# Splitting the last layer's values on GpSimd, so that eleven sums over adj run as three float32r passes

## The reference, cut to what matters

```python
h = jnp.maximum(_layernorm(x, axis=-1), 0.0)
# W: (3, 128, 128)
h = jnp.einsum('bjf,kfo->kbjo', x, W)             # three values per node; x is the h above
out = (jnp.einsum('ij,bjo->bio', adj_0, h[0])     # adj_0: the diagonal
     + jnp.einsum('ij,bjo->bio', adj_1, h[1])     # adj_1: triu(adj, 1)
     + jnp.einsum('ij,bjo->bio', adj_2, h[2]))    # adj_2: tril(adj, -1)
return out + bias[None, None, :]
```

## Time and profile before

| what | value |
|---|---|
| median of 3 runs | 405.15 us |
| the profiled execution's own time | 404.75 us |
| its span, first to last instruction | 402.8 us |
| TensorE matmul busy | 396.2 us (98%) |
| VectorE busy | 346.2 us (86%) |
| ScalarE busy | 287.3 us (71%) |
| GpSimd busy | 41.0 us (10%) |
| granted TensorE clock | 1.000 |

### The profile page before, as it was taken

The page is one execution under the profiler, slowest core; times in us unless marked ns, Lnnn a source line. Parts: engine busy times, 40 slices in busy tenths (PEclk is TensorE's granted clock), DMA queues, the critical chain, the costliest instruction groups (busy, mean ns, idle before and its releaser), DMA issues.

```text
span 402.8 us, 6585 instructions
## 1 busy us (share of the span) xinstructions
PE 396.2 (98%) x2404; PEld 348.0 (86%) x2404; DVE 346.2 (86%) x872; ACT 287.3 (71%) x579; POOL 41.0 (10%) x43
## 2 busy tenths in 40 slices
PE   8999999999999999999999999999999999999997
PEld 8787889898887889899777879899797788989896
DVE  6568999997989898887998898989798979787897
ACT  4767775685798676777689676777689767766554
POOL 4910003000200003000110000300030000000130
PEclk9999999999999999999999999999999999999999
DMA  7920000000000000000000000000000000000003
GB/s 229 317 110 2 1 0 2 1 2 0 2 1 2 27 28 0 28 0 2 3 0 26 28 0 28 0 28 1 2 2 26 0 28 26 2 26 2 1 2 130
DMA packets 5215, 11.18 MB, mean 28 GB/s; under 512 B 1088, under 2 KB 2112, under 8 KB 4672
## 3 DMA queue, kind: packets, MB, share of 16 engines
q1 hardware_dynamic: 5184, 10.77, 7.6%
HBM read 6.57 MB, written 4.19 MB: 27 GB/s over the span
## 4 chain that ended last, share of the span: by engine, by line
PE 81%; DVE 13%; ACT 5%; issue 1%; POOL 0%; DVEq 0%; ACTq 0%; POOLq 0%
PE PS L514 11%; PE PS L523 11%; PE PS L515 10%; PE PS L546 6%; PE PS L543 6%; PE PS L542 6%; PE PS L592 4%; PE PS L440 4%; PE PS L463 4%; PE PS L473 4%; PE PS L455 4%; PE PS L581 3%; PE PS L582 2%; PE PS L583 2%; ACT GT L849 2%; ACT TC L855 2%
## 5 line engine op out<-in xcount | busy, mean ns | idle before, releaser
L849 ACT ACTIVATE GT<-PS,BG 128x256 f32<-128x256 f32 (+2 forms) x312 | 157.8, 563 | 16.5 <-PE PS L546 12.4
L514 PE MATMUL PS<-HH,WIH 128*128 128x256 f32 (+2 forms) x312 | 107.3, 345 | 1.8 <-DVE HH L1000 1.7
L515 PE MATMUL PS<-HH,WIL 128*128 128x256 f32 (+2 forms) x312 | 102.7, 330 | 0.0
L523 PE MATMUL PS<-HL,WIH 128*128 128x256 f32 (+2 forms) x294 | 97.3, 331 | 0.5
L855 ACT ACTIVATE TC<-CS 128x512 f32<-128x512 f32 (+2 forms) x88 | 45.2, 514 | 49.5 <-DVE CS L976 36.2
L514 PEld LDWEIGHTS PS<-HH,WIH 128*128 128x128 f32 x312 | 58.8, 188 | 11.5 <-DVE HH L1007 4.3
L382 POOL TENSOR_TENSOR RS<-VE,NHALF 128x4 f32<-128x4 f32 (+2 forms) x17 | 29.2, 1718 | 351.0 <-DVE VE L921 272.7
L515 PEld LDWEIGHTS PS<-HH,WIL 128*128 128x128 f32 x312 | 58.9, 189 | 3.9 <-issue 1.2
L523 PEld LDWEIGHTS PS<-HL,WIH 128*128 128x128 f32 x294 | 55.5, 189 | 6.6 <-DVE HL L1015 2.4
L546 PE MATMUL PS<-SL,WHH 128*128 128x256 f32 (+2 forms) x192 | 60.1, 313 | 0.1
L542 PE MATMUL PS<-SH,WHH 128*128 128x256 f32 (+2 forms) x192 | 59.9, 312 | 0.0
(11 more groups left out here) (97 smaller groups left out, 657.5 us busy)
## 6 DMA issues: line engine op xcount, KB each, us to landing
out_tbd<-X SPq DMA_DIRECT2D x15, 256.0 KB, 2.0
X<-x_tbd SPq DMA_DIRECT2D x3, 1024.0 KB, 13.2
X<-x_tbd SPq DMA_DIRECT2D x4, 256.0 KB, 4.2
WI<-wih_t SPq DMA_DIRECT2D x1, 1024.0 KB, 6.1
WH<-whh_t SPq DMA_DIRECT2D x1, 768.0 KB, 7.6
out_tbd<-X SPq DMA_DIRECT2D x2, 128.0 KB, 1.7
WL<-w_l SPq DMA_DIRECT2D x1, 192.0 KB, 6.7
WG<-wg SPq DMA_DIRECT2D x2, 64.0 KB, 3.4
```

Of the source, the lines that this page charges most:

```text
L514: pe.matmul(dst, WIH[:, p - 1, cols], x_high, start=True, stop=False)
L515: pe.matmul(dst, WIL[:, p - 1, cols], x_high, start=False, stop=False)
L523: mm = pe.matmul(dst, WIH[:, p - 1, cols], x_low, start=False, stop=(j == 0))
L849: act.activation(GT[:, s, q, 0:n], bank(s, q)[:, 0:n], ACT.Tanh if q == C else ACT.Sigmoid, bias=BG[:, 4 * (p - 1) + q:4 * (p - 1) + q + 1 ...
```

## The change

In the eleven quads for which `sums_split` is true (all of groups 0 and 1, quads 0 to 2 of group 2), the values of sides 1 and 2 are split by GpSimd into a float32r high part VH (a copy) and a low part VL (value minus high), value by value after its copy out of PSUM. The triangles of adj are split once in the same way into ADJH and ADJL. A SUM then is six float32r matmuls of 512 columns (high by ADJH and by ADJL for both sides, then low by ADJH for both sides) instead of two float32 ones. It waits for `value_high` of the quad's last value before the first four and for `value_low` before the last two. In GpSimd's order, eleven splits stand before the `rstd` of the first layer and five behind it; in the last group twelve splits stand before the four `rstd` calls. The triangles are built later, after ScalarE's and VectorE's late weight split, since ADJ2 now lies in a free part of WI; BIASH lies in VH. The other five quads stay plain float32.

```diff
+def sums_split(g, q):
+    return g < GROUPS - 2 or (g == GROUPS - 2 and q < LAST)
+def splits_before(g, n):
+    return G * g + n
+SPLIT_FIRST = 11
...
-            pool.wait_ge(consts, 4)
             pool.wait_ge(w_adj, 16)
-            for k, sign in enumerate((1, -1)):
-                pool.affine_select(out=ADJ2[:, k, :], in_=ADJ[:, :], ...)
             pool.wait_ge(w_ih, 16)
...
+            pool.wait_ge(consts, 4)
+            pool.wait_ge(late_low, LATE_ORDER.index("wi") + 1)
+            for k, sign in enumerate((1, -1)):
+                pool.affine_select(out=ADJ2[:, k, :], in_=ADJ[:, :], ...)
+            pool.wait_ge(consts, 6)
+            pool.tensor_copy(ADJH[:, :, :], ADJ2[:, :, :]).then_inc(side_parts, 1)
+            pool.wait_ge(side_parts, 1)
+            pool.tensor_tensor(ADJL[:, :, :], ADJ2[:, :, :], ADJH[:, :, :].bitcast(F32),
+                               ALU.subtract).then_inc(side_parts, 1)
+            def split_value(g, n):
+                full, high, low = value_sides(n)
+                pool.wait_ge(value_sb, G * g + n + 1)
+                pool.tensor_copy(high, full).then_inc(value_high, 1)
+                pool.wait_ge(value_high, splits_before(g, n) + 1)
+                pool.tensor_tensor(low, full, high.bitcast(F32), ALU.subtract).then_inc(value_low, 1)
             def group(i):
+                for n in range(SPLIT_FIRST) if i > 0 else ():
+                    split_value(i - 1, n)
                 rstd(VE1, var1, 2 * (QUARTERS + i + 1), RS1, rs1, 0, G)
+                for n in range(SPLIT_FIRST, G) if i > 0 else ():
+                    split_value(i - 1, n)
...
             i = GROUPS - 1
+            for n in range(LAST * PACK):
+                split_value(i - 1, n)
             for q in range(QUADS):
...
             def last_sum(g, q, ps, lo=0, hi=PACK):
+                if not sums_split(g, q):
+                    for k in range(SIDES):
+                        last_side(g, q, k, ps, lo, hi)
+                    return
+                pe.wait_ge(value_high, splits_before(g, q * PACK + hi))
                 for k in range(SIDES):
-                    last_side(g, q, k, ps, lo, hi)
+                    high = VH[:, k, lo * D:hi * D]
+                    pe.matmul(ps[:, lo * D:hi * D], ADJH[:, k, :], high, start=(k == 0), stop=False)
+                    pe.matmul(ps[:, lo * D:hi * D], ADJL[:, k, :], high, start=False, stop=False)
+                pe.wait_ge(value_low, splits_before(g, q * PACK + hi))
+                for k in range(SIDES):
+                    mm = pe.matmul(ps[:, lo * D:hi * D], ADJH[:, k, :], VL[:, k, lo * D:hi * D],
+                                   start=False, stop=(k == SIDES - 1))
+                mm.then_inc(out_mm, 1)
```

More of the change, by code:

```diff
@@ L190, in program @@
         ADJ = sb("ADJ", [T, T])
-        ADJ2 = sb("ADJ2", [T, SIDES, T])
+        ADJH = sb("ADJH", [T, SIDES, T], F32R)
+        ADJL = sb("ADJL", [T, SIDES, T], F32R)
+        VH = sb("VH", [T, SIDES, PACK * D], F32R)
+        VL = sb("VL", [T, SIDES, PACK * D], F32R)
         DIAG = sb("DIAG", [T, 1])
@@ L201, in program @@
         BIAS = sb("BIAS", [T, D])
-        BIASH = sb("BIASH", [T, D], F32R)
         BIAS2 = sb("BIAS2", [T, D], F32R)
@@ L220, in program @@
         NHALF = sb("NHALF", [T, G])
+        ADJ2 = WI[:, POOL_SKIPS, 0:SIDES * T].rearrange("p (k t) -> p k t", k=SIDES)
+        BIASH = VH[:, 0, 0:D]
         PS = ctx.enter_context(nc.psum_tensor("PS", [128, 8, 512], F32))
@@ L275, in program @@
         value_sb = sem("value_sb")
+        side_parts = sem("side_parts")
+        value_high = sem("value_high")
+        value_low = sem("value_low")
         own_ready = sem("own_ready")
@@ L314, in values, with value_sides @@
             return (WI, WH)[q % 2]
+        def value_sides(n):
+            q, b = divmod(n, PACK)
+            cols = slice(b * D, b * D + D)
+            return values(q)[:, 1:PARTS, cols], VH[:, :, cols], VL[:, :, cols]
         def quad(q):
@@ L389, in _ @@
                 pool.tensor_tensor(SHIFT1[:, part], MINUS1[:, part], RS1[:, part], ALU.mult).then_inc(shift1, 1)
-            pool.wait_ge(consts, 4)
             pool.wait_ge(w_adj, 16)
-            for k, sign in enumerate((1, -1)):
-                pool.affine_select(out=ADJ2[:, k, :], in_=ADJ[:, :], compare_op=ALU.is_gt, fill=0.0,
-                                   base=0, pattern=[[-sign, T]], channel_multiplier=sign).then_inc(consts, 1)
             pool.wait_ge(w_ih, 16)
@@ L412, in _ @@
                     done += 1
+            pool.wait_ge(consts, 4)
+            pool.wait_ge(late_low, LATE_ORDER.index("wi") + 1)
+            for k, sign in enumerate((1, -1)):
+                pool.affine_select(out=ADJ2[:, k, :], in_=ADJ[:, :], compare_op=ALU.is_gt, fill=0.0,
+                                   base=0, pattern=[[-sign, T]], channel_multiplier=sign).then_inc(consts, 1)
+            pool.wait_ge(consts, 6)
[9 more added lines that the diff above has]
+                pool.tensor_tensor(low, full, high.bitcast(F32), ALU.subtract).then_inc(value_low, 1)
             def group(i):
+                for n in range(SPLIT_FIRST) if i > 0 else ():
+                    split_value(i - 1, n)
                 rstd(VE1, var1, 2 * (QUARTERS + i + 1), RS1, rs1, 0, G)
+                for n in range(SPLIT_FIRST, G) if i > 0 else ():
+                    split_value(i - 1, n)
                 for s in range(STREAMS):
@@ L672, in _ @@
             pe.wait_ge(bias_parts, 3)
+            pe.wait_ge(side_parts, 2)
             for i in range(1, GROUPS - 1):
```

## The result

The changed kernel takes 414.46 us (median; 414.21 to 414.67), the kernel before 405.05 us beside it: ratio 1.0233, 95% interval 1.0222 to 1.0243. Slower by 9.4 us, where +4.2 us were forecast. The span grew from 402.8 to 412.6 us, and the granted clock is 1.0 in both.

A forecast was written before the change was run, and what follows sets the result against it. TensorE was taken as the bound on average (98% busy), partly waiting for VectorE. Delays of 2.85 + 1.05 + 1.0 less 0.7 gained gave +4.2 us: 408.95, as a median 409.4 us; range 402.8 to 414.0.

The forecast's parts named there:

- the triangles: adj's later triangles on GpSimd fall into group 0, needed by TensorE some 50 us later: no cost.
- value 11: Split at 256.5 to 257.7, held back by the pow, where VectorE runs gapless into unit 13's chain: 1.0 us lost.
- rival C: VectorE pays full price, whole-instruction turns, 0.9 us and more a value: +11, 416 us; chance 0.05.
- The price of a value: VectorE delay per split value from GpSimd's streaming: 0.65 x 0.81 = 0.5 us.
- SUM -1's gain: Shorter float32r sum on TensorE's path, twice 0.35 us: 0.7 us gained, kept because it comes ahead of the delays.
- the late chain behind SUM 1: Value 7's split runs beside VectorE's L1015 and L1072, delaying L967, the chain's head: 0.35 x 3 = 1.05 us lost.
- values 0 to 3: Splits between 212.3 and 218.5 delay VectorE's L1063, which VALUE 4 waits for: 2.85 us lost over three groups.
- Rival B: GpSimd always yields, some 2.5 us a value, so TensorE waits in SUM 0 for the low part: about 411; chance 0.08.
- The other values meet units whose hidden parts are 2 us early: 0: Splits of values outside the named places were to delay nothing TensorE waits for: 0 us.
- The undisturbed CAST at 253.72: VectorE's CAST kept its usual 0.34 us during GpSimd's 128x16 pow; taken as evidence against whole-instruction blocking and rival C.

The follow-up runs named there:

- the run with the last quads: Changed kernel with triangles split early, but only values 12 to 15 of the first two groups split and only their two closing sums in three passes: 405.61 us.

## Why the prediction was wrong

The direction held, and that VectorE is what is held back, and three of the terms. What failed is the placing of these delays: the forecast set the values that it did not name (4 to 6, 8 to 10 and 12 to 15) and the triangles at nothing, and value 11 at half. The time, 414.46 us, lies nearer to rival C (416) than to the forecast (409.4), and C's mechanism, turns by whole instructions, is the one that the traces show, at 0.5 us a value and not C's 0.9. Point by point:

- **The price of a value: right.** "0.5 us of VectorE delay a value" was taken; VectorE's busy time grew by 22.2 / 44 = 0.50 us. The reason given (the streaming parts overlap 65% of the time) was not what happens. The engines take turns by whole instructions, and what a turn costs goes by how far apart two starts happen to be; that the two come to the same number is luck.
- **SUM -1's gain, the late chain behind SUM 1, values 0 to 3: right** (-0.7, 1.05 and 2.85 forecast; -0.7, 1.2 and 3.1 measured). TensorE also waited some 0.36 us (by the starts) in front of SUM 0 for the high part of value 3, which was to be 0.3 us early: GpSimd was slowed as well, and a value took it 1.5 us on average (1.21 to 2.00), not 1.2. Rival B was there, in small, but this wait added nothing: behind SUM 0, VALUE 4 still waits for VectorE's L1118, and in the run with the splits alone, where no sum waits, the delay from TURN 1 to VALUE 4 grows by the same 0.65 us. The changed kernel, TensorE and then VectorE:

```profile
223.34 0.47 PE L648 MATMUL PS<-VH,ADJH 128*128 128x512 f32 x1 [0.20 <-POOL VH L446]
...
225.97 0.41 PE L623 MATMUL PS<-WLH,HTH 128*128 128x384 f32 x1 [0.29 <-DVE HTL L1118]
...
225.15 0.68 DVE L1118 SCALAR_TENSOR_TENSOR HTL<-PS,HTH 128x512 fp32r<-128x512 f32 x1
```

- **"The other values meet units whose hidden parts are 2 us early: 0" failed**, and is the largest part: 1.9 + 1.3 = 3.2 us. It looked only at the hidden parts and not at what else TensorE asks of VectorE. At gate F of unit 6 it waits for ADD 0, which frees SUM 0's bank. The changed kernel, VectorE and then TensorE:

```profile
227.72 0.89 DVE L1136 SCALAR_TENSOR_TENSOR X<-WI,DIAG,X 128x512 f32<-128x512 f32 x1
228.52 1.23 DVE L1019 TENSOR_TENSOR CS<-GT 128x512 f32<-128x512 f32 x1
229.67 0.68 DVE L1145 TENSOR_TENSOR X<-PS,X 128x512 f32<-128x512 f32 x1
...
230.41 0.50 PE L556 MATMUL PS<-HH,WIH 128*128 128x512 f32 x1 [0.36 <-DVE X L1145]
```

  The add itself keeps its 0.68 us. What delays it is queued in front of it: 0.15 + 0.54 us on two instructions beside value 4's split. And at the end of a group the delay from values 12 to 15 stays in the loop between VectorE and ScalarE until the next group's layers, where TensorE has no slack, as the run with the last quads shows.
- **Value 11: right place, half the size** (1.0 forecast, 2.3 measured, for two groups). The split comes right behind the `pow`, so do VectorE's two scalings of L982, which waited for the same `pow`. The changed kernel:

```profile
263.26 0.50 POOL L446 CAST VH<-WI 128x256 fp32r<-128x256 f32 x1
263.84 0.74 POOL L448 TENSOR_TENSOR VL<-WI,VH 128x256 fp32r<-128x256 f32 x1
...
263.42 1.24 DVE L982 TENSOR_SCALAR H<-X,MINUS,RS 128x128 f32<-128x128 f32 x2
264.59 0.49 DVE L1058 TENSOR_TENSOR HF<-GT,TC 128x336 f32<-128x336 f32 x1
...
265.51 0.38 PE L556 MATMUL PS<-HH,WIH 128*128 128x256 f32 x1 [0.48 <-DVE HH L1062]
```

  The pair took 0.60 us before. It pays for the copy and for the subtraction: 0.64 us. An average price was used where the two engines were started by the same event, which makes the collision certain. The other 0.5 us of each group's 1.15 arise in the chain behind it; no run isolated them, and their cause stays open.
- **The triangles "cost none": failed by 0.6 us.** TensorE does not need them for long, but VectorE's chain runs beside them: HT 0.66 us (0.51 before) and the CAST behind it 0.74 (0.33). The run with early triangles gave back 0.60. The changed kernel there:

```profile
56.57 0.40 POOL L437 CAST ADJH<-WI 128x256 fp32r<-128x256 f32 x1
57.05 0.86 POOL L439 TENSOR_TENSOR ADJL<-WI,ADJH 128x256 fp32r<-128x256 f32 x1
...
56.67 0.66 DVE L1058 TENSOR_TENSOR HT<-GT,TC 128x336 f32<-128x336 f32 x1
57.36 0.74 DVE L1062 CAST SH<-HT 128x336 fp32r<-128x336 f32 x1
```

- **The undisturbed CAST at 253.72 was misread.** It was the argument against whole-instruction turns, and so for giving rival C only 0.05. The CAST ran inside a `pow` on 16 columns. The same CAST in the changed kernel takes 0.74 us beside the triangles' split, so it can be held. What that `pow` shows is only that a 3.09 us instruction over 16 columns does not hold it; why not, no run here settles. It was a poor stand-in for an instruction that reads 256 columns.

The sum: 3.2 (other values) + 1.3 (value 11) + 0.6 (triangles) + 0.5 (small excesses of the terms that held, start and end) = 5.6 us, the 9.8 of the ledger less the 4.2 forecast.

## What to carry to other kernels

An idle GpSimd is not free for work that reads SBUF while a VectorE that reads SBUF is near the path: count the extra VectorE time (here 0.5 us for each 1.1 us of GpSimd work), and then lay it at every place where TensorE waits for anything of VectorE, a freed bank or the next layer included, not only at the chain that the profile shows as late. What costs is the length of one reading instruction against the gap between VectorE's starts: copies of 0.40 us were nearly free (88 of them, two a value: 405.99 us), a subtraction of 0.73 was not. Before moving work to a second engine, ask whether the event that starts it also starts the engine it disturbs.

## What the runs showed of the hardware

- GpSimd's copies and subtractions take turns with VectorE's products, casts and scalings from SBUF to SBUF, by whole instructions: VectorE's 128x512 product ends 0.54 to 0.56 us after GpSimd's instruction does, for instructions of 0.48, 0.69 and 0.80 us, with one input or two. VectorE's statistics (279 ns) were not held inside a subtraction, nor anything inside the `pow` on 16 columns (3.09 us).
- GpSimd's writes take no turn that VectorE feels: with 44 memsets of 0.72 us the kernel took 404.18 us.
- VectorE's instructions with an input in PSUM kept 0.68 us beside all of this (six started inside a half subtraction with about 0.40 us of it left); its CAST from SBUF to SBUF did not (0.33 to 0.74 us at worst).
- Halving GpSimd's instructions spares VectorE (834 to 759 ns) and costs GpSimd: a pair of 128x128 subtractions took 0.88 to 1.66 us, the one of 128x256 0.73 to 1.07.
